# Moving chunk 3's first layer norm behind the first half's scaled queries in a convolution and attention kernel

## The chip, the cores and the metric

The kernel runs on one core of a Trainium2 chip. The metric is device time in microseconds of one execution. A core has TensorE (matrix multiply, with a queue of its own for weight loads), VectorE, ScalarE and GpSimd, and the sync engine, which here only starts transfers. Each engine works through its own list of instructions in the order in which they are written and waits for the others on semaphores.

## The reference

Two blocks in a row on x of shape (32, 32, 16, 16): 32 images of 32 channels and 16 x 16 pixels. The first block, cut to what matters here:

```python
def _biasfree_ln(x, w):
    mu = jnp.mean(x, axis=1, keepdims=True)
    var = jnp.mean((x - mu) ** 2, axis=1, keepdims=True)
    return x / jnp.sqrt(var + EPS) * w[None, :, None, None]

def _elgca_attn(x, dw_w, dw_b, qkvl_w, qkvl_b):
...
    x1, x2 = (x[:, :C2], x[:, C2:])
    x1 = _gelu(_conv(x1, dw_w, dw_b, groups=C2, pad=1))
    x2 = _gelu(_conv(x2, qkvl_w, qkvl_b))
    x2 = x2.reshape(B, HEADS, C4, H, W)
    q = jnp.sum(x2[:, :HEADS - 3], axis=1)
    k = x2[:, HEADS - 3]
    v = x2[:, HEADS - 2].reshape(B, C4, H * W)
    lfeat = x2[:, HEADS - 1]
    qf = _avg_pool_3s2p1(q).reshape(B, C4, -1)
    kf = _max_pool_2s2(k).reshape(B, C4, -1)
    qk = jnp.einsum('bcn,bdn->bcd', qf, kf)
    attn = jnp.swapaxes(jax.nn.softmax(qk, axis=1), 1, 2)
    out = jnp.einsum('bcd,bdn->bcn', attn, v).reshape(B, C4, H, W)
    return jnp.concatenate([x1, lfeat, out], axis=1)
...
h = _biasfree_ln(x, ln1_w)
h = _elgca_attn(h, dw_w, dw_b, qkvl_w, qkvl_b)
out = h + x
m = _biasfree_ln(out, ln2_w)
m = _elgca_mlp(m, fc1_w, fc1_b, pos_w, pos_b, fc2_w, fc2_b)
return out + m
```

Here C2 is 16 and C4 is 8: a 3x3 depthwise convolution of one half of the channels beside a 1x1 projection of the other half into q, k, v and lfeat. The MLP is a 1x1 to 128 channels, a depthwise 3x3 added to it, and a 1x1 back. The second block is attention over the 256 pixels of each image (32 channels, softmax over the query axis) with a residual.

## The kernel before

The 32 images lie as four groups of eight: partition = group x 32 + channel, and eight **slots** of 256 pixels along the free axis. Two slots are a **chunk** (0 to 3; 512 columns, one PSUM bank wide), and two chunks are a **half** H (0: slots 0 to 3, 1: slots 4 to 7). All is in 32-bit floats. PSUM is used as eight banks: LOW is banks 0 to 3, HIGH is 4 to 7.

Nothing schedules the work: each engine's list is written out by hand, and the semaphores carry the order between engines. The stages around the change are these.

- `centre(0, k, banks)` and `variance(0, k, banks)` (L286, L297) are 32x32 matmuls with a constant matrix. Each serves one chunk: four groups times two slots, 8 matmuls. TensorE then uses 8 of its 16 tiles of 32 x 32, since group g and slot s go to row tile g and column tile (g + s) mod 4 (for the variance the other way round).
- ScalarE squares the centred values (`square`, L707), and in `inverse_root` (L713, L716) takes a logarithm and then an exponential with scale -0.5, which gives 1/sqrt(var + eps). Both need the table set `exp_tables`; GELU needs `gelu_tables`, and each change of set is an ACT_TABLE_LOAD.
- VectorE multiplies (`normalise_input`, L879) into the padded buffer `npad`, raising the semaphore `normed[0]` by one for each slot, and splits the result by pixel parity (`split_parities`, L887).
- `qk(k, bank)` (L306) projects a chunk's queries and keys with full 128x128 matmuls, and `qk_act` (L720) applies GELU for one half at a time. `pool_queries` (L343) is the average pool as a matmul, `scale_queries` (L724) divides by 9, and `pool_keys` (L896) is the max pool on VectorE.
- `channel_scores` (L356) gives the channel attention's scores. `softmax_in` (L906, L907), `channel_exp` on ScalarE (L729) and `softmax_out` (L914 to L919) give the mixing weights `mix_w`.
- The depthwise convolution with the v and lfeat projections runs as taps: `attn_singles` (L317) for taps 4, 3 and 5, straight from `npad`, and `attn_pairs` (L331) for the six others in pairs, from a copy `npairs` that the sync engine's queue makes (`place_pairs`, which waits for `normed[0]` of the whole half). `attn_act` (L733) is their GELU, and `mix(H, banks)` (L369) combines all. `residual` (L926) adds x, and the second layer norm begins with `centre(1, ...)` (L286 again).

Every matmul of 32-bit floats stands in the trace as two records; so one tap for four slots (16 matmuls) is 32 records, on all 16 tiles.

ScalarE's order in this stretch is

```python
            inverse_root(0, 2, HIGH)
            inverse_root(0, 3, HIGH)
            act.preload_act_table_set(gelu_tables)
            qk_act(0, 4)
            act.preload_act_table_set(exp_tables)
            scale_queries(0, 5)
            channel_exp(0)
            act.preload_act_table_set(gelu_tables)
```

The channel scores of half 0 lie in banks 5 and 6. Bank 6 also holds chunk 3's variance, so that TensorE waits for chunk 3's logarithm (`log_ready[0]`, 4) ahead of them.

## Time and profile before

| | |
|---|---|
| median of 3 runs | 112.94 us (112.91 to 114.23) |
| profiled execution, its own time | 113.05 us |
| its span, first to last instruction | 111.3 us |
| TensorE matmul busy | 95.7 us, 86% |
| TensorE weight loads busy | 53.9 us, 48% |
| ScalarE busy | 86.2 us, 77% |
| VectorE busy | 76.3 us, 69% |
| GpSimd busy | 11.7 us, 11% |
| mean granted TensorE clock | 0.995 |

The span leaves 1.75 us of the execution's own time outside it. Busy shares are means over the whole span; the change lies in a stretch of some 15 us near its start, and what bounds that stretch is read from the timelines and the chain of waits. Overlapping matmuls make TensorE look busier than it is: in the timeline a group's time runs to the end of its last matmul, and the next group may start some hundredths earlier.

### The profile page before, as it was taken

The numbers are of one execution on the slowest core, as the hardware profiler recorded it, in microseconds if no ns is written. First come the engines' busy times: TensorE is split into PE (matmuls) and PEld (weight loads), VectorE is DVE, ScalarE is ACT, GpSimd is POOL, SyncE is SP. The second block draws the span as 40 slices with busy tenths as digits, with TensorE's granted clock in tenths as the row PEclk, the third lists the DMA queues.
The fourth block names the chain that finished last, engine by engine and source line by source line (L and its number), as shares of the span: only waits on it lengthen the run. The fifth ranks groups of instructions, "written<-read, shape, count | busy, mean of one in ns | idle before, by whom it ended". The sixth has DMA issues, their size and how long they took to land.

```text
span 111.3 us, 5328 instructions
## 1 busy us (share of the span) xinstructions
PE 95.7 (86%) x2424; PEld 53.9 (48%) x2424; DVE 76.3 (69%) x155; ACT 86.2 (77%) x203; POOL 11.7 (11%) x25
## 2 busy tenths in 40 slices
PE   0097699999969999989987999999999999997660
PEld 0023286865425567324443653576624665585320
DVE  0002997554749897999879889567471789889751
ACT  4048897797989639896569899869999868979950
POOL 7010000000000000000000003692000030004200
PEclk9999999999999999999999999999999999999998
DMA  2991053200000000000000000000000200020022
GB/s 53 229 377 52 0 219 112 119 0 6 6 0 9 0 9 6 0 6 6 0 6 0 6 6 0 0 6 6 6 0 6 94 0 6 0 93 4 0 95 99
DMA packets 2070, 4.56 MB, mean 41 GB/s; under 512 B 384, under 2 KB 640, under 8 KB 2048
## 3 DMA queue, kind: packets, MB, share of 16 engines
q1 hardware_dynamic: 1904, 4.20, 10.6%
q8 instruction: 19, 0.31, 1.2%
q10 hardware_dynamic: 144, 0.03, 0.2%
q14 instruction: 3, 0.02, 0.1%
HBM read 1.96 MB, written 1.05 MB: 27 GB/s over the span
## 4 chain that ended last, share of the span: by engine, by line
PE 62%; ACT 22%; DVE 6%; DMA 4%; issue 3%; ACTq 0%; DVEq 0%
PE ps L398 19%; ACT prob L787 5%; PE ps L488 5%; ACT hpad L738 5%; PE ps L446 4%; DMA first<-first_in 4%; PE ps L498 4%; PE ps L518 4%; PE ps L481 3%; ACT prob L774 3%; PE ps L415 3%; PE ps L286 3%; PE ps L382 3%; PE ps L423 2%; ACT swapped L733 2%
## 5 line engine op out<-in xcount | busy, mean ns | idle before, releaser
L398 PE MATMUL ps<-hpad,third 32*32 32x450 f32 (+2 forms) x864 | 38.9, 563 | 0.1
L787 ACT ACTIVATE prob<-ps,smax 128x256 f32<-128x256 f32 x56 | 25.7, 477 | 3.8 <-DVE smax L999 3.7
L952 DVE SCALAR_TENSOR_TENSOR unit<-hpad,third,unit 128x544 f32<-128x544 f32 x32 | 23.5, 789 | 0.0
L999 DVE TENSOR_REDUCE smax<-ps 128x2 f32<-128x512 f32 x26 | 16.6, 685 | 4.7 <-PE ps L498 2.9
L398 PEld LDWEIGHTS ps<-hpad,third 32*32 32x32 f32 x864 | 15.1, 103 | 8.7 <-issue 4.5
L263 POOL TENSOR_TENSOR v_tok<-v_tok,row_inv 128x256 f32<-128x256 f32 x7 | 4.7, 677 | 87.8 <-DVE row_inv L1009 87.8
L787 ACT ACTIVATION_READ_ACCUMULATOR prob<-ps,smax 128x1 f32 x56 | 11.7, 209 | 0.0
L738 ACT ACTIVATE hpad<-ps,third 128x1024 f32<-128x1024 f32 x8 | 8.7, 1116 | 2.9 <-PE ps L382 2.4
L879 DVE SCALAR_TENSOR_TENSOR npad<-x,first,rstd 128x256 f32<-128x256 f32 x8 | 3.5, 480 | 10.3 <-ACT rstd L716 10.3
L518 PE MATMUL ps<-prob,v_tok 128*32 128x256 f32 x128 | 8.2, 383 | 2.3 <-ACT prob L774 1.1
L707 ACT ACTIVATE swapped<-ps 128x512 f32<-128x512 f32 x8 | 4.5, 593 | 7.2 <-PE ps L286 7.2
L498 PE MATMUL ps<-rstd,swapped 32*32 32x256 f32 x192 | 8.9, 383 | 0.6 <-ACT prob L787 0.6
L286 PE MATMUL ps<-x,first 32*32 32x256 f32 x64 | 3.8, 628 | 5.7 <-DMA first<-first_in 5.7
L488 PE MATMUL ps<-rstd,swapped 32*128 32x256 f32 x80 | 7.3, 397 | 0.3 <-DVE rstd L969 0.3
L747 ACT ACTIVATE acc<-ps,third 128x512 f32<-128x512 f32 x12 | 7.3, 688 | 0.2 <-PE ps L398 0.2
L498 PEld LDWEIGHTS ps<-rstd,swapped 32*32 32x32 f32 x192 | 4.9, 103 | 4.2 <-ACT prob L787 2.9
L518 PEld LDWEIGHTS ps<-prob,v_tok 128*32 128x32 f32 x128 | 3.9, 109 | 6.4 <-issue 2.8
L446 PE MATMUL ps<-X,third 32*32 32x256 f32 x128 | 6.9, 381 | 0.0
L297 PE MATMUL ps<-swapped,first 32*32 32x256 f32 x128 | 5.2, 446 | 1.6 <-ACT swapped L707 1.5
L713 ACT ACTIVATE rstd<-ps,eps_col 128x512 f32<-128x512 f32 x8 | 5.4, 676 | 1.5 <-PE ps L297 1.5
L488 PEld LDWEIGHTS ps<-rstd,swapped 32*128 32x128 f32 x80 | 5.1, 184 | 2.7 <-issue 1.2
L382 PE MATMUL ps<-m,third 32*32 32x512 f32 x64 | 4.4, 598 | 1.1 <-ACT hpad L738 0.9
(87 smaller groups left out, 145.1 us busy)
## 6 DMA issues: line engine op xcount, KB each, us to landing
prob<-npad SPq DMA_DIRECT2D x4, 297.5 KB, 2.5
x<-x_in SPq DMA_DIRECT2D x4, 256.0 KB, 5.6
y<-m SPq DMA_DIRECT2D x3, 256.0 KB, 2.5
third<-third_in SPq DMA_DIRECT2D x1, 456.5 KB, 6.8
second<-second_in SPq DMA_DIRECT2D x1, 401.5 KB, 5.8
y<-m SPq DMA_DIRECT2D x2, 128.0 KB, 2.0
first<-first_in ACTq DMA_DIRECT2D x1, 33.0 KB, 4.9
```

What stands on the lines that cost most here:

```text
L286: last = pe.matmul(ps[quadrant(rotated(g, s)), banks[s % 4], 0:NPIX], c1("centre")[quadrant(g), :], slot((x, res1)[ln], s)[quadrant(g), :] ...
L382: last = pe.matmul(ps[quadrant(c), bank, :], c3("fc1_w")[quadrant(g), c * C:(c + 1) * C], m[quadrant(g), k, :], start=True, stop=True)
L398: last = pe.matmul(inside(pixels(ps[quadrant(rotated(r, g)), banks[g], :]), tap), c3("taps")[quadrant(r), tap * C:(tap + 1) * C], inside(p ...
L446: last = pe.matmul(ps[quadrant(rotated(g, s)), bank, half * NPIX:(half + 1) * NPIX], c3(w)[quadrant(g), :], slot(X, s)[quadrant(g), :], st ...
L488: last = pe.matmul(ps[:, banks[q], jt * NPIX:(jt + 1) * NPIX], slot(swapped, s)[quadrant(q), jt * P:(jt + 1) * P], slot(rstd, s)[quadrant( ...
L498: last = pe.matmul(ps[quadrant(c), banks[q], jt * NPIX:(jt + 1) * NPIX], slot(swapped, s)[quadrant(q), at:at + C], slot(rstd, s)[quadrant( ...
L518: last = pe.matmul(ps[quadrant(g), bank, 0:NPIX], v_tok[:, s, at:at + C], prob[:, G * (slot_turn(s) % PROBS) + g, jt * NPIX:(jt + 1) * NPI ...
L738: act.activation(padded(hpad, h_first(k, g), 4, CENTRE), two(banks).rearrange("p g (t y s) -> p (g t) y s", t=2, s=SIDE), ACT.Gelu, bias=c ...
L747: act.activation(acc_buf(k, g), ps[:, banks[g], :], ACT.Gelu, bias=c3("pos_b")[:, g:g + 1]).then_inc(conv_gelu, 1)
L787: last = act.activation(prob[:, G * (slot_turn(s) % PROBS) + g, jt * NPIX:(jt + 1) * NPIX], ps[:, banks[q], jt * NPIX:(jt + 1) * NPIX], AC ...
L952: dve.scalar_tensor_tensor(out=sums, in0=source, scalar=weight, in1=sums, op0=ALU.mult, op1=ALU.add).then_inc(unit_step, 1)
L999: dve.tensor_reduce(smax[:, s, 2 * q:2 * q + 2], ps[:, banks[q], :].rearrange("p (j i) -> p j i", j=2), AX_X, ALU.max, negate=True).then_i ...
```

## The change

Chunk 3's `inverse_root` moves on ScalarE from ahead of the first GELU table load to behind `scale_queries(0, 5)`. VectorE takes chunk 3's `normalise_input` and `split_parities` behind `softmax_in(0)`. TensorE's list changes in four ways: the single taps of half 0 are split in two by slots (0 and 1, then 2 and 3, by the new argument `slots`); those of slots 0 and 1 for taps 4 and 3 come ahead of the variances of chunks 2 and 3; the pairs of half 0 all come behind the channel scores; and the wait for chunk 3's logarithm stands ahead of `qk(2, 7)`. The channel scores of half 0 use banks 4 and 5. No instruction is added or dropped, and there are as many table loads as before.

```diff
--- before.py
+++ after.py
@@ -307,11 +307,11 @@
                                      c2("qk_w"), start=True, stop=True)
                 last.then_inc(qk_proj, 1)
 
-            def attn_singles(H, lo, hi, banks):
+            def attn_singles(H, lo, hi, banks, slots=range(G)):
 
                 for i in range(lo, hi):
                     tap = ATTN_SINGLES[i]
-                    for t in range(G):
+                    for t in slots:
                         s = G * H + t
                         for g in range(G):
                             pe.matmul(inside(pixels(ps[quadrant(rotated(g, s)), banks[t], 0:NPIX]), tap),
@@ -531,21 +531,23 @@
             centre(0, 2, HIGH)
             pe.wait_ge(x_loaded[3], 16)
             centre(0, 3, HIGH)
+            pe.wait_ge(second_loaded, 16)
+            pe.wait_ge(normed[0], 2)
+            attn_singles(0, 0, 2, LOW, (0, 1))
             variance(0, 2, HIGH)
             variance(0, 3, HIGH)
-            pe.wait_ge(second_loaded, 16)
-            pe.wait_ge(normed[0], 4)
-            attn_singles(0, 0, 1, LOW)
+            attn_singles(0, 2, 3, LOW, (0, 1))
             pe.wait_ge(log_ready[0], 3)
             qk(0, 4)
             qk(1, 4)
-            attn_singles(0, 1, 3, LOW)
+            pe.wait_ge(normed[0], 4)
+            attn_singles(0, 0, 2, LOW, (2, 3))
             pool_queries(0, 5)
-            attn_pairs(0, 0, 1, LOW)
+            attn_singles(0, 2, 3, LOW, (2, 3))
+            pe.wait_ge(kf_zeroed, 1)
+            channel_scores(0, (4, 5))
+            attn_pairs(0, 0, 3, LOW)
             pe.wait_ge(log_ready[0], 4)
-            pe.wait_ge(kf_zeroed, 1)
-            channel_scores(0, (5, 6))
-            attn_pairs(0, 1, 3, LOW)
             qk(2, 7)
             qk(3, 7)
             mix(0, LOW)
@@ -801,11 +803,11 @@
             square(0, 2, HIGH)
             square(0, 3, HIGH)
             inverse_root(0, 2, HIGH)
-            inverse_root(0, 3, HIGH)
             act.preload_act_table_set(gelu_tables)
             qk_act(0, 4)
             act.preload_act_table_set(exp_tables)
             scale_queries(0, 5)
+            inverse_root(0, 3, HIGH)
             channel_exp(0)
             act.preload_act_table_set(gelu_tables)
             act.wait_ge(second_loaded, 16)
@@ -1013,7 +1015,7 @@
                 dve.tensor_tensor(slot(m, s), ps[:, bank, 0:NPIX], slot(X, s), ALU.add).then_inc(y_ready, 1)
 
             dve.wait_ge(first_loaded, 16)
-            for k in range(CHUNKS):
+            for k in range(CHUNKS - 1):
                 dve.wait_ge(x_loaded[k], 16)
                 normalise_input(k)
                 if k == 0:
@@ -1021,7 +1023,10 @@
                 split_parities(k)
             dve.wait_ge(kf_zeroed, 1)
             pool_keys(0)
-            softmax_in(0, (5, 6))
+            softmax_in(0, (4, 5))
+            dve.wait_ge(x_loaded[3], 16)
+            normalise_input(3)
+            split_parities(3)
             dve.wait_ge(blocks_zeroed, 1)
             dve.wait_ge(mix_preset, 1)
             softmax_out(0)
```

How the lists look, first **TensorE** from the variances of chunks 2 and 3 (L297) on; L317 are single taps, L306 the projections, L343 the pooling of the queries, L331 the pairs. Before:

```order
15 L297 MATMUL ps<-swapped,first 32x256 [waits squared0]
16 L297 MATMUL ps<-swapped,first 32x256 x7
17 L317 MATMUL ps<-npad,second 32x256 [waits normed0,second_loaded]
18 L317 MATMUL ps<-npad,second 32x256 x15
19 L306 MATMUL ps<-second,parity 128x64 [waits parity_split,log_ready0]
20 L306 MATMUL ps<-second,parity 128x64 x3
21 L306 MATMUL ps<-second,parity 128x64 [waits parity_split]
22 L306 MATMUL ps<-second,parity 128x64 x3
23 L317 MATMUL ps<-npad,second 32x16x15 x32
24 L343 MATMUL ps<-qk_tok,second 128x64 [waits qk_gelu]
25 L343 MATMUL ps<-qk_tok,second 128x64 x3
26 L331 MATMUL ps<-prob,second 32x16x15 [waits pairs_placed0]
```

With the change:

```order
13 L317 MATMUL ps<-npad,second 32x256 [waits normed0,second_loaded]
14 L317 MATMUL ps<-npad,second 32x256 x7
15 L317 MATMUL ps<-npad,second 32x16x15 x8
16 L297 MATMUL ps<-swapped,first 32x256 [waits squared0]
17 L297 MATMUL ps<-swapped,first 32x256 x7
18 L297 MATMUL ps<-swapped,first 32x256 [waits squared0]
19 L297 MATMUL ps<-swapped,first 32x256 x7
20 L317 MATMUL ps<-npad,second 32x16x15 x8
21 L306 MATMUL ps<-second,parity 128x64 [waits parity_split,log_ready0]
22 L306 MATMUL ps<-second,parity 128x64 x3
23 L306 MATMUL ps<-second,parity 128x64 [waits parity_split]
24 L306 MATMUL ps<-second,parity 128x64 x3
```

Sixteen single-tap matmuls (two taps of two slots) now stand ahead of the variances, and eight more (the third tap) behind them, ahead of the projections L306; the wait for `normed0` that opens them is now for two slots and not for four. The list goes on:

```order
25 L317 MATMUL ps<-npad,second 32x256 [waits normed0]
26 L317 MATMUL ps<-npad,second 32x256 x7
27 L317 MATMUL ps<-npad,second 32x16x15 x8
28 L343 MATMUL ps<-qk_tok,second 128x64 [waits qk_gelu]
29 L343 MATMUL ps<-qk_tok,second 128x64 x3
30 L317 MATMUL ps<-npad,second 32x16x15 x8
31 L356 MATMUL ps<-qf,kf 32x8 [waits q_scaled,k_pooled,kf_zeroed]
32 L356 MATMUL ps<-qf,kf 32x8 x15
33 L331 MATMUL ps<-prob,second 32x16x15 [waits pairs_placed0]
34 L331 MATMUL ps<-prob,second 32x16x15 x15
```

The other two slots' singles stand around the pooling L343, and all 48 pair matmuls follow the channel scores L356; before, 16 of them stood ahead of the scores.

**ScalarE** from chunk 2's logarithm on (L713 and L716 before are L715 and L718 with the change, and L720, L724, L729, L733 become L722, L726, L731, L735). Before:

```order
10 L713 ACTIVATE rstd<-ps,eps_col 128x512 [waits var_ready0]
11 L716 ACTIVATE rstd<-rstd 128x512 [waits log_ready0]
12 L713 ACTIVATE rstd<-ps,eps_col 128x512 [waits var_ready0]
13 L716 ACTIVATE rstd<-rstd 128x512 [waits log_ready0]
14 L805 ACT_TABLE_LOAD
15 L720 ACTIVATE qk_tok<-ps 128x512 [waits qk_proj]
16 L807 ACT_TABLE_LOAD
17 L724 ACTIVATE qf<-ps 128x64 [waits q_pooled]
18 L729 ACTIVATE att<-att 128x32 [waits att_shifted]
```

With the change:

```order
10 L715 ACTIVATE rstd<-ps,eps_col 128x512 [waits var_ready0]
11 L718 ACTIVATE rstd<-rstd 128x512 [waits log_ready0]
12 L806 ACT_TABLE_LOAD
13 L722 ACTIVATE qk_tok<-ps 128x512 [waits qk_proj]
14 L808 ACT_TABLE_LOAD
15 L726 ACTIVATE qf<-ps 128x64 [waits q_pooled]
16 L715 ACTIVATE rstd<-ps,eps_col 128x512 [waits var_ready0]
17 L718 ACTIVATE rstd<-rstd 128x512 [waits log_ready0]
18 L731 ACTIVATE att<-att 128x32 [waits att_shifted]
```

One logarithm and one exponential have moved from ahead of the first table load to behind the scaled queries.

**VectorE** from chunk 3's normalisation (L879 before, L881 with the change) on. Before:

```order
13 L879 SCALAR_TENSOR_TENSOR npad<-x,first,rstd 128x16x16 [waits rstd_ready0,x_loaded3]
14 L879 SCALAR_TENSOR_TENSOR npad<-x,first,rstd 128x16x16
15 L887 TENSOR_SCALAR parity<-npad,second 128x128 [waits normed0]
16 L887 TENSOR_SCALAR parity<-npad,second 128x128 x3
17 L896 TENSOR_REDUCE kf<-qk_tok 128x4x8 [waits qk_gelu,kf_zeroed]
18 L896 TENSOR_REDUCE kf<-qk_tok 128x4x8
19 L906 TENSOR_REDUCE att_max<-ps 128x4 [waits att_scores]
20 L907 TENSOR_TENSOR att<-ps,att_max 128x32 [waits dve_chain]
21 L914 TENSOR_REDUCE att_sum<-att 128x4 [waits att_exp,mix_preset,blocks_zeroed]
```

With the change:

```order
13 L898 TENSOR_REDUCE kf<-qk_tok 128x4x8 [waits qk_gelu,kf_zeroed]
14 L898 TENSOR_REDUCE kf<-qk_tok 128x4x8
15 L908 TENSOR_REDUCE att_max<-ps 128x4 [waits att_scores]
16 L909 TENSOR_TENSOR att<-ps,att_max 128x32 [waits dve_chain]
17 L881 SCALAR_TENSOR_TENSOR npad<-x,first,rstd 128x16x16 [waits rstd_ready0,x_loaded3]
18 L881 SCALAR_TENSOR_TENSOR npad<-x,first,rstd 128x16x16
19 L889 TENSOR_SCALAR parity<-npad,second 128x128 [waits normed0]
20 L889 TENSOR_SCALAR parity<-npad,second 128x128 x3
21 L916 TENSOR_REDUCE att_sum<-att 128x4 [waits att_exp,mix_preset,blocks_zeroed]
```

Chunk 3's two multiplications and four splits now stand between the softmax's subtraction and its sum (L914 before, L916 with the change), so `mix_w` waits for them.

## Rows read from the trace of the kernel before

**Rows 1.** The chain of work that ended last, in order of time, 10 to 32 us (start us, us, what)

```profile
17.39 1.03 PE ps L343 x8
...
23.06 0.73 PE ps L369 x32
```

**Rows 2.** ScalarE's timeline, 10 to 31 us (start us, us, engine line op out<-in xcount)

```profile
12.72 0.69 ACT L713 ACTIVATE rstd<-ps,eps_col 128x512 f32<-128x512 f32 x1 [0.34 <-PE ps L297]
...
13.97 0.67 ACT L713 ACTIVATE rstd<-ps,eps_col 128x512 f32<-128x512 f32 x1
...
15.32 1.28 ACT L805 ACT_TABLE_LOAD   x1
16.62 0.60 ACT L720 ACTIVATE qk_tok<-ps 128x512 f32<-128x512 f32 x1
...
18.53 0.22 ACT L724 ACTIVATE qf<-ps 128x64 f32<-128x64 f32 x1
20.11 0.23 ACT L729 ACTIVATE att<-att 128x32 f32<-128x32 f32 x1 [1.36 <-DVE att L907]
...
21.65 1.26 ACT L733 ACTIVATE swapped<-ps,second 128x512 f32<-128x512 f32 x2
22.84 0.60 ACT L720 ACTIVATE qk_tok<-ps 128x512 f32<-128x512 f32 x1
```

**Rows 3.** TensorE's timeline, 11 to 24 us (same columns)

```profile
11.95 1.15 PE L297 MATMUL ps<-swapped,first 32*32 32x256 f32 x32 [1.45 <-ACT swapped L707]
13.37 0.73 PE L317 MATMUL ps<-npad,second 32*32 32x256 f32 x32 [0.26 <-DVE npad L879]
14.02 2.00 PE L306 MATMUL ps<-second,parity 128*128 128x64 f32 x16
15.95 1.44 PE L317 MATMUL ps<-npad,second 32*32 32x240 f32 x64
...
18.36 0.69 PE L331 MATMUL ps<-prob,second 32*32 32x240 f32 x32
19.11 0.37 PE L356 MATMUL ps<-qf,kf 64*32 64x8 f32 x32
19.41 1.47 PE L331 MATMUL ps<-prob,second 32*32 32x256 f32 x64
20.80 2.00 PE L306 MATMUL ps<-second,parity 128*128 128x64 f32 x16
```

**Rows 4.** VectorE's timeline, 10 to 31 us

```profile
10.32 0.88 DVE L879 SCALAR_TENSOR_TENSOR npad<-x,first,rstd 128x256 f32<-128x256 f32 x2 [10.32 <-ACT rstd L716]
...
16.24 0.87 DVE L879 SCALAR_TENSOR_TENSOR npad<-x,first,rstd 128x256 f32<-128x256 f32 x2
17.15 1.12 DVE L887 TENSOR_SCALAR parity<-npad,second 128x128 f32<-128x128 f32 x4
...
20.47 0.18 DVE L914 TENSOR_REDUCE att_sum<-att 128x4 f32<-128x32 f32 x1 [0.39 <-ACT att L729]
...
21.47 0.18 DVE L919 COPY mix_w<-att_turned 128x32 f32<-128x32 f32 x1
23.47 0.65 DVE L896 TENSOR_REDUCE kf<-qk_tok 128x32 f32<-128x128 f32 x2 [1.81 <-ACT qk_tok L720]
```

**Rows 5.** TensorE's timeline around two groups of L446, 88.8 to 90 and 93.89 to 95 us

```profile
88.88 1.07 PE L446 MATMUL ps<-X,third 32*32 32x256 f32 x16
...
93.90 1.12 PE L446 MATMUL ps<-X,third 32*32 32x256 f32 x32
```

**Rows 6.** DMA issues by line (KB each, median us to landing), and the second half's first pairs on TensorE

```profile
prob<-npad SPq DMA_DIRECT2D x4, 297.5 KB, 2.5
...
30.50 0.78 PE L331 MATMUL ps<-prob,second 32*32 32x240 f32 x32
```

**Rows 7.** TensorE's timeline, 24 to 29.5 us

```profile
26.96 0.42 PE L317 MATMUL ps<-npad,second 32*32 32x256 f32 x4
27.03 0.42 PE L297 MATMUL ps<-swapped,first 32*32 32x256 f32 x8
```

## The prediction

> **What bounds the kernel now.** I read the chain of waits first. From 10 to 25 us it runs along TensorE's list, and the two rows in [rows 1] are what a reader should see of it: the query pooling and the mixing matmuls each start when TensorE comes to them or when ScalarE releases them, with no slack to speak of. Then the timelines. ScalarE's shows that the first GELU (16.62) waits for its table load (15.32 + 1.28), and that load stands behind chunk 3's logarithm and exponential, which take from 13.97 to 15.32, so 1.35 us [rows 2]. That is what the change takes out of the way. TensorE's shows groups almost end to end: from the first projection at 14.02 to the end of the second pair of projections, 20.80 + 2.00 = 22.80, there is no hole of even 0.1 us except around the channel scores [rows 3]. ScalarE's second GELU then starts at 22.84 [rows 2]. So two engines are nearly late together: whatever ScalarE gives, TensorE's list must be able to take.
>
> **Step 1, the early single taps.** They need only chunk 0's normalisation, which ends at 10.32 + 0.88 = 11.20 [rows 4]. With the 0.15 that the mixing matmuls took to follow ScalarE's end (21.65 + 1.26 = 22.91 to 23.06) [rows 1, 2] they start at 11.35, in a hole that lasts until the variances at 11.95 [rows 3]. The group is 32 records, but on two slots, so on 8 tiles. The nearest rows: 32 records on 8 tiles of the same width took 1.12, and 16 records on 4 tiles took 1.07 [rows 5]. The double work costs nothing more, so it is the four records in a row on each tile that set the time: 0.26 each (1.05 to the start of what follows; these groups overlap the next by some 0.07). On all 16 tiles 64 records, again four on a tile, took 1.44, or 1.38 to the next group's start (15.95 to 18.36 less the pooling's 1.03) [rows 1, 3]. So the early group holds its tiles until about 12.40, and 0.45 of that is behind the point where chunk 2's variance could start. It shares four tiles with it. Bounds: no delay of the variance (its other tiles are free), or 0.85 (it waits for the whole group, priced at 1.44). I take 0.3: four records and then two of the variance on a tile are 6 x 0.26 = 1.56 from 11.35, 12.91 and a tail of 0.1, against the variance's end just ahead of the logarithm at 12.72 [rows 2]. Chunk 2's logarithm then starts at 13.03.
>
> A page bears on this. The Trainium skill, "TensorEngine Tiling (Array Packing)", Theoretical Speedup, has 32 x 32 tiles bring up to 16 times, so half the tiles in use is half the speed. That speaks against splitting the taps by slots. Taken literally from the 16-tile rows (0.34 a round and not 0.26) it would add 8 x 0.08 = 0.6 to the groups below; the trace shows a half-used array at 0.26 a round, so it agrees in direction and not in full size.
>
> **Step 2, the projections.** They wait for chunk 2's logarithm, 13.03 + 0.69 = 13.72, so start at 13.85, not 14.02; the third tap of slots 0 and 1 (16 records, two rounds) fits ahead, since the busiest tile has 8 rounds from 11.35, to 13.45. They take 15.95 - 14.02 = 1.93 [rows 3] and TensorE is free at 15.78. ScalarE: exponential to 14.38, table load to 15.68, GELU at 15.88 when the projections' last has ended, not 16.62 [rows 2]. So of 1.35 taken off ScalarE 0.74 arrives; TensorE keeps the rest.
>
> **Step 3, the pooling and the scores.** Ahead of the pooling stand the singles of slots 2 and 3, 32 records on 8 tiles, 1.05: to 16.83. GELU is done at 16.48, so the pooling is bound by TensorE: 16.83 and not 17.33 (0.50 of gain left). It ends at 17.87 after 1.03 [rows 1]. The third tap of these slots takes 0.55 (two rounds and a small gap), where 0.75 stood (18.36 to 19.11) [rows 3]; the scaled queries are ready at 17.97 + 0.22 = 18.19 [rows 2] and hide behind it. Scores at 18.42, not 19.11: gain 0.69. Their move to banks 4 and 5 costs nothing: both banks' readers, GELU and the scaling, are done before; if they kept banks 5 and 6, they would wait for the moved logarithm.
>
> **Step 4, where TensorE gives it back.** All pairs now follow the scores: 96 records where 64 took 20.80 - 19.41 = 1.39 and 32 took 0.65 to 0.75 [rows 3], so 2.05. Scores' 0.30, then 18.75 + 2.05 = 20.80. The second half's projections start at the same 20.80 as before. The whole gain on TensorE has gone into taps that now run on half the tiles.
>
> **Step 5, the new wait.** Chunk 3's layer norm: ScalarE takes it at 18.21 (its set of tables is the one loaded there, so no load is added) and ends 1.35 later, 19.56. `channel_exp`, queued behind it, is ready at 19.42 (before, it started at 20.11, which is 1.00 behind the scores' start) [rows 2, 3], so it is held by 0.14 and still far ahead of 20.11. VectorE starts chunk 3's normalisation at 19.70. From there to the end of the splits is 17.15 + 1.12 - 16.24 = 2.03 [rows 4]: 21.73. Two things wait for that. First `qk(3, 7)`: with the handover and a weight load it starts at 21.9, where TensorE would be ready at 21.77, and ends at 22.95, not 22.80. Second `softmax_out(0)`, now behind the splits on VectorE: 20.47 to 21.65 is 1.18 [rows 4], so `mix_w` is ready at 22.83, not 21.65; the mixing matmuls are behind the projections anyway, 22.95, so it hides by 0.1. If that cover goes it costs one for one. `attn_act` runs from 21.13 to 22.39 and is not late. The second GELU starts at 22.98, not 22.84: a loss of 0.14. VectorE's key pooling (23.47) [rows 4] follows it, then the residual and the second layer norm's centring, so all move by that 0.14.
>
> **Step 6, the rest.** The sync queue's copy for the second half's pairs waits for chunk 3, from 20.6 and not 17.1. With 2.5 to land and two issues it is there by about 25; its reader comes at 30.50 [rows 6], so it costs nothing. From 25 us on the lists are the same, and the shift goes through. Sum: +0.15 on an execution of 113.05, so 113.2; that execution lay 0.1 over the median of 112.94. **Forecast: 113.1.**
>
> **The rivals.** All of them lie inside 2%, which is about what a measurement of this kernel can tell from no change.
>
> *Faster: half-used tiles cost by the record.* If small groups keep the 16-tile price of 0.02 a record (0.65 for 32) [rows 3] and the variance is not held, the logarithm stays at 12.72, the third tap is done at 13.4, the projections end at 15.5 (VectorE's splits of chunk 1 bound them) and the pooling starts right behind GELU at 16.3. Chunk 3's norm then starts at 17.73, its splits end at 21.25, and the second GELU starts at 22.53: -0.3, so 112.6. For it: the change does take 1.35 us from the binding table load. Against it: 16 records on 4 tiles cost as much as 32 on 8 [rows 5].
>
> *Slower: the early taps hold up the variance.* If chunk 2's variance starts only when the 32 early records are through, and these cost 16-tile rounds, it starts at 11.35 + 1.44 = 12.79, and the logarithm at 13.55. From a logarithm at 13.2 on each hundredth moves the projections and all that follows, in the end chunk 3's splits: +0.5 on the forecast, so 113.6. Against it: in a like place matmuls of two lines are in the array together, L317 at 26.96 ahead of L297's last at 27.03, though L297 stands first in the list [rows 7]. The Trainium skill, "TensorE: Matmul & The Clock Gate", Part 3, has matmuls start and end strictly in order, and this rival is what such a queue would do here; the rows just named speak against it.
>
> *No effect of its own.* The order of instructions shows that the logarithm has left the place ahead of the table load, so that the change does nothing is not left open; what could change by another amount is the second half of the kernel, where I assume a plain shift.
>
> **How the numbers follow.** Forecast 0.50, with its own range 112.9 to 113.4; faster rival 0.23; slower rival 0.23; something else, beyond either, 0.04. The range runs from the one rival to the other with 0.15 to 0.2 on each side for the scatter between runs (112.91, 112.94, and 113.05 in the profile): 112.4 to 113.8. Over 2% faster would be under 110.7, over 2% slower over 115.2; no case reaches them, and the 0.04 is split: 0.01, 0.97, 0.02.
>
> **What would show it.** Right, if the profile of the changed kernel has the early singles at 11.3 to 11.4, chunk 2's logarithm near 13.0, the first GELU near 15.9 right behind the projections and no longer behind its table load, the pooling near 16.8 with no wait for GELU, the second half's projections near 20.8, a VectorE that sums the softmax only at 21.6, and the second GELU near 23.0. The rivals part at two rows: the logarithm (12.7 or 13.5) and the time of 32 singles on two slots (0.7 or 1.4 for my 1.1). I would be wrong if the pairs behind the scores took clearly less than 2.05, if `mix_w` and not the projections released the mixing, or if the shift at 25 us were not the shift at the end.

## The result, and the profile after

The changed kernel took 112.53 us (median of 20 executions, 112.06 to 113.87) against 113.56 for the kernel before (median of 20, 112.50 to 122.22). The ratio is 0.9948, with a 95% interval of 0.9925 to 0.9971: 0.6 us faster, between 0.3 and 0.9. That ratio leaves out executions that lie far over the fastest of their kernel; the medians keep them, and what is known of them is told with the experiments. By the bound of 2% this is no change. The profiled execution took 112.90 us with a span of 111.1.

The two spans can't be set against each other directly. The first loads land when they land: the first normalisation on VectorE starts at 10.32 in the trace before [rows 4] and at 9.54 in the one after. So times below are also given as **offsets** from that start, and the **stretch** is the time from it to the first fc1 GELU on ScalarE (L738 before, L740 after), 10.32 to 30.96 before, so 20.64.

ScalarE's timeline after the change, which answers to [rows 2]:

```profile
12.16 0.69 ACT L715 ACTIVATE rstd<-ps,eps_col 128x512 f32<-128x512 f32 x1 [0.56 <-PE ps L297]
...
13.53 1.28 ACT L806 ACT_TABLE_LOAD   x1
14.93 0.60 ACT L722 ACTIVATE qk_tok<-ps 128x512 f32<-128x512 f32 x1
...
16.96 0.22 ACT L726 ACTIVATE qf<-ps 128x64 f32<-128x64 f32 x1
17.08 0.68 ACT L715 ACTIVATE rstd<-ps,eps_col 128x512 f32<-128x512 f32 x1
...
21.77 0.60 ACT L722 ACTIVATE qk_tok<-ps 128x512 f32<-128x512 f32 x1 [0.57 <-PE ps L306]
...
29.89 2.12 ACT L740 ACTIVATE hpad<-ps,third 128x1024 f32<-128x1024 f32 x2
```

The table load now starts at 13.53, right behind chunk 2's exponential, and ends at 14.81; GELU at 14.93 waits for the projections and no longer for the load. Chunk 3's logarithm comes at 17.08, behind the scaled queries. The stretch is 29.89 - 9.54 = 20.35, so 0.29 shorter.

TensorE's timeline, which answers to [rows 3]:

```profile
10.56 1.05 PE L317 MATMUL ps<-npad,second 32*32 32x256 f32 x29 [0.90 <-DVE npad L881]
11.25 0.40 PE L297 MATMUL ps<-swapped,first 32*32 32x256 f32 x1
...
11.29 0.82 PE L297 MATMUL ps<-swapped,first 32*32 32x256 f32 x22
11.83 0.36 PE L317 MATMUL ps<-npad,second 32*32 32x240 f32 x1
...
12.90 2.00 PE L306 MATMUL ps<-second,parity 128*128 128x64 f32 x16 [0.17 <-ACT rstd L715]
14.82 1.07 PE L317 MATMUL ps<-npad,second 32*32 32x256 f32 x32
15.82 1.11 PE L343 MATMUL ps<-qk_tok,second 128*128 128x64 f32 x8
...
17.73 2.07 PE L331 MATMUL ps<-prob,second 32*32 32x240 f32 x96
19.74 2.00 PE L306 MATMUL ps<-second,parity 128*128 128x64 f32 x16
21.71 0.73 PE L369 MATMUL ps<-swapped,mix_w 32*32 32x256 f32 x32
```

A reader should see the early taps (L317 at 10.56) with the variances (L297, from 11.25 on) pushed in among their last (L317 at 11.83, which stands ahead of them in the list), and then groups end to end from 12.90 to 21.71. The 32 records on two slots take 1.00 to the next group's start (14.82 to 15.82), the 96 pairs 2.01 (17.73 to 19.74), and the mixing matmuls start when the second pair of projections is through.

VectorE's timeline, which answers to [rows 4]:

```profile
9.54 0.88 DVE L881 SCALAR_TENSOR_TENSOR npad<-x,first,rstd 128x256 f32<-128x256 f32 x2 [9.54 <-ACT rstd L718]
...
18.53 0.88 DVE L881 SCALAR_TENSOR_TENSOR npad<-x,first,rstd 128x256 f32<-128x256 f32 x2 [0.17 <-ACT rstd L718]
19.44 1.12 DVE L889 TENSOR_SCALAR parity<-npad,second 128x128 f32<-128x128 f32 x4
...
21.47 0.18 DVE L921 COPY mix_w<-att_turned 128x32 f32<-128x32 f32 x1
```

Chunk 3 is normalised at 18.53, its splits end at 19.44 + 1.12 = 20.56, and `mix_w` is ready at 21.65, 0.06 before the mixing matmuls at 21.71: it hides, barely.

One more row matters. At 75 us the changed kernel's lead over the trace before was 1.07 (0.78 of it from the earlier loads), and ten us later it was 0.15. In between stands this row of TensorE's:

```profile
75.82 0.37 PE L498 MATMUL ps<-rstd,swapped 32*32 32x256 f32 x1 [0.47 <-issue]
```

The hole of 0.47 before this row is put down to nothing that the profile shows ("issue"). Whether it belongs to the change is what the second experiment asks.

### The profile page after: what moved, and what is told of

Read it like the earlier page. It is cut to its first block, busy times and chain, and to the rows that moved or that the text cites. A ratio compares the mean times of both kernels' runs of the same rounds, so it can differ in the third digit from the quotient of the medians.

```text
span 111.1 us, 5328 instructions
## 1 busy us (share of the span) xinstructions
PE 96.8 (87%) x2424; PEld 54.4 (49%) x2424; DVE 76.4 (69%) x155; ACT 86.2 (78%) x203; POOL 11.7 (11%) x25
## 3 DMA queue, kind: packets, MB, share of 16 engines
HBM read 1.96 MB, written 1.05 MB: 27 GB/s over the span
## 4 chain that ended last, share of the span: by engine, by line
PE 64%; ACT 21%; DVE 5%; DMA 4%; issue 2%; SPq 0%; ACTq 0%; DVEq 0%
PE ps L398 18%; PE ps L498 5%; ACT prob L789 5%; PE ps L488 5%; ACT hpad L740 5%; PE ps L446 4%; DMA x<-x_in 4%; PE ps L518 4%; PE ps L306 4%; PE ps L481 3%; ACT prob L776 3%; PE ps L415 3%; PE ps L286 3%; PE ps L382 3%; PE ps L317 2%
## 5 line engine op out<-in xcount | busy, mean ns | idle before, releaser
L398 PEld LDWEIGHTS ps<-hpad,third 32*32 32x32 f32 x864 | 14.6, 103 | 9.9 <-issue 5.8
L740 ACT ACTIVATE hpad<-ps,third 128x1024 f32<-128x1024 f32 x8 | 8.7, 1115 | 2.9 <-PE ps L382 2.4
L881 DVE SCALAR_TENSOR_TENSOR npad<-x,first,rstd 128x256 f32<-128x256 f32 x8 | 3.5, 482 | 9.7 <-ACT rstd L718 9.7
L317 PE MATMUL ps<-npad,second 32*32 32x240 f32 (+1 forms) x192 | 6.3, 373 | 0.9 <-DVE npad L881 0.9
L446 PE MATMUL ps<-X,third 32*32 32x256 f32 x128 | 6.9, 381 | 0.0
L715 ACT ACTIVATE rstd<-ps,eps_col 128x512 f32<-128x512 f32 x8 | 5.4, 677 | 1.3 <-PE ps L297 1.3
L297 PE MATMUL ps<-swapped,first 32*32 32x256 f32 x128 | 5.7, 446 | 0.0
```

Source lines behind the costliest of these rows:

```text
L317: pe.matmul(inside(pixels(ps[quadrant(rotated(g, s)), banks[t], 0:NPIX]), tap), c2("attn_taps")[quadrant(g), i * C:(i + 1) * C], inside(pa ...
L398: last = pe.matmul(inside(pixels(ps[quadrant(rotated(r, g)), banks[g], :]), tap), c3("taps")[quadrant(r), tap * C:(tap + 1) * C], inside(p ...
L446: last = pe.matmul(ps[quadrant(rotated(g, s)), bank, half * NPIX:(half + 1) * NPIX], c3(w)[quadrant(g), :], slot(X, s)[quadrant(g), :], st ...
L740: act.activation(padded(hpad, h_first(k, g), 4, CENTRE), two(banks).rearrange("p g (t y s) -> p (g t) y s", t=2, s=SIDE), ACT.Gelu, bias=c ...
```

## The experiments

All ratios are to runs of the kernel before that were taken beside each kernel on the same chip; that chip was not the same for all of them. Of the edits the lines that matter are shown, and "..." marks what is left out.

**The two kernels again.** No edit.

> The kernel before, unchanged, to see how far one profile of it lies from the next. I measure a stretch inside the profile, from the start of chunk 0's normalisation on VectorE to the start of the first fc1 GELU on ScalarE: 10.32 to 30.96, so 20.64 us in the trace of before, and 9.54 to 29.89, so 20.35, with the change. If that stretch is what the change acts on, it repeats here at 20.6 within 0.05, the ratio is 1.00, and the first normalisation may start anywhere from 9.5 to 10.4, as the first loads land. The rival, that the stretch itself scatters by some tenths, would show another length here.

Ratio 1.0011 (0.9962 to 1.0059). The stretch was 21.32, not 20.64, so the rival has a point; two rows of TensorE's timeline show where:

```profile
18.86 1.72 PE L331 MATMUL ps<-prob,second 32*32 32x256 f32 x64
...
29.24 0.66 PE L317 MATMUL ps<-npad,second 32*32 32x240 f32 x20 [0.64 <-issue]
```

The second group of pairs took 1.72 where [rows 3] has 1.47, and the second half's single taps waited 0.64 for nothing visible. Offsets up to the channel scores are those of before within 0.01. The traces of the later experiments settle the rest. Four with the old order have a stretch of 20.63 to 20.65 (`before`, `before_late_copy`, `before_filled`, `before_filled2`), and four with the new order have 20.34 to 20.36 (`after`, `ctl_after2`, `after_warm`, `after_filled_warm`). So the stretch repeats to 0.02, but for stops of TensorE that come in some executions, and the new order is worth 0.29 in it.

> The changed kernel, unchanged. Stretch 20.35 again within 0.05; time 0.3 to 0.6 us under before. The profile of the change had a hole of 0.47 us on TensorE near 75.4 us that nothing explains, and the lead over before shrank there from 1.07 to 0.15. If that belongs to the new order of instructions it comes back here in the same place; if it is an accident of one execution it is gone, and this profile's span is about 0.8 us shorter from the first fc1 GELU to the end (81.2 in that profile, 80.3 in before's).

Ratio 0.9954 (0.9919 to 0.9988). Every offset up to the residual is that of the first trace after within 0.02. The hole at 75 us is gone: from the first fc1 GELU to the end 80.3, as before. So it does not come in every execution of the changed kernel, but it was no accident of one either: the trace of `after_late_copy`, told below, waits 0.44 for nothing visible ahead of the same instruction, 45.90 behind its first fc1 GELU (45.93 in the first trace after), and has 81.2 from there to the end, as that one had. The hole stands in 2 of 12 traces of kernels with any part of the change and in none of 6 without; that doesn't tell whether the change has a part in it. A smaller stop (0.41, in the second half's singles) made this stretch 20.56.

**One part of the change alone.** In the first kernel TensorE keeps the old order of taps and pairs, and ScalarE's and VectorE's lists are the new ones (the edit is to the changed kernel):

```diff
             centre(0, 3, HIGH)
-            pe.wait_ge(second_loaded, 16)
-            pe.wait_ge(normed[0], 2)
-            attn_singles(0, 0, 2, LOW, (0, 1))
             variance(0, 2, HIGH)
             variance(0, 3, HIGH)
...
+            attn_pairs(0, 0, 1, LOW)
             pe.wait_ge(kf_zeroed, 1)
             channel_scores(0, (4, 5))
-            attn_pairs(0, 0, 3, LOW)
+            attn_pairs(0, 1, 3, LOW)
```

> ScalarE's and VectorE's part of the change alone (and the banks and the later wait for the logarithm), with TensorE's taps in the old order. My theory: TensorE was nearly as late as ScalarE, so the GELU starts 0.5 earlier but the pooling does not, while chunk 3's norm now ends behind the scaled queries: splits end near 22.3 on the clock of the trace of before, second GELU near 23.4. The stretch is 0.5 to 0.7 longer than before's 20.64, time +0.5 to +0.7 us. Rival (ScalarE alone bounded the stage, the new tap order is of no use): the stretch is as short as with the whole change, 20.35, time -0.3 or better.

Ratio 1.003 (0.9992 to 1.0069): the gain is gone, as my theory has it, and the rival's 0.997 is excluded. The loss, 0.3 us, is under the 0.5 to 0.7 that I gave, and the interval includes 1.000. Its one profiled execution took 121.31 us, so that the forecast stretch was never seen undisturbed, and its granted clock says why (us, PE, PEld, DVE, ACT, POOL busy, PEclk, DMA share, GB/s):

```profile
10.00:12.00 2.00, 0.44 (x16) 0.18 (x16) 1.89 (x7) 1.96 (x4) 0.00 (x0) 1.00 0.04 8
12.00:14.00 2.00, 1.96 (x57) 0.50 (x48) 1.96 (x8) 1.62 (x3) 0.00 (x0) 0.59 0.00 0
14.00:24.00 10.00, 10.00 (x200) 7.50 (x185) 3.08 (x11) 4.41 (x7) 0.00 (x0) 0.50 0.16 63
...
38.00:40.00 2.00, 1.59 (x40) 0.37 (x36) 0.58 (x1) 1.99 (x2) 0.00 (x0) 1.00 0.00 0
```

The clock fell from 1.00 to 0.50, from 2.4 to 1.2 GHz, soon after 12 us and was not back until 36. Its matmuls show it, 1.17 and 3.67 where [rows 3] has 0.73 and 2.00:

```profile
12.98 1.17 PE L317 MATMUL ps<-npad,second 32*32 32x256 f32 x32
14.08 3.67 PE L306 MATMUL ps<-second,parity 128*128 128x64 f32 x16
```

In the second kernel ScalarE's and VectorE's lists are the old ones and TensorE's is the new one (again an edit to the changed kernel; VectorE's part is not shown):

```diff
             inverse_root(0, 2, HIGH)
+            inverse_root(0, 3, HIGH)
             act.preload_act_table_set(gelu_tables)
...
             scale_queries(0, 5)
-            inverse_root(0, 3, HIGH)
```

> TensorE's new order and banks 4 and 5 alone, with chunk 3's norm at its old place on ScalarE and VectorE. My theory: the early taps delay chunk 2's logarithm by 0.22 and with it the table load, and the pairs behind the scores come late: second GELU 0.5 to 0.7 later than before, time +0.5 to +0.7 us, so each part alone loses and only the two together gain. Rival (the early use of the hole is where the gain is from): the stretch is shorter than 20.64, time -0.2 or better.

Its stretch is 21.25, 0.61 longer than before's, as forecast. ScalarE's timeline:

```profile
12.32 0.69 ACT L715 ACTIVATE rstd<-ps,eps_col 128x512 f32<-128x512 f32 x1 [0.56 <-PE ps L297]
...
14.93 1.28 ACT L807 ACT_TABLE_LOAD   x1
16.22 0.60 ACT L722 ACTIVATE qk_tok<-ps 128x512 f32<-128x512 f32 x1
...
22.84 0.60 ACT L722 ACTIVATE qk_tok<-ps 128x512 f32<-128x512 f32 x1 [0.56 <-PE ps L306]
```

GELU again sits behind its table load, now 0.22 later by offset (6.52 for 6.30), and the second GELU is 0.62 later (13.14 for 12.52). But the time was only 1.0014 (0.9985 to 1.0043), where I had said 0.5 to 0.7 us more: 0.16 more, 0.45 better than its own stretch would have it. Its 12 executions lay within 0.7 us, where before's spread over 10. Its lowest is 113.16, 0.9 over before's lowest, 112.26; it is the others of before that are slower than its rows would have them. Something else than the order of the work had got better. It has the early taps.

**When the sync queue's copy starts.** A wait ahead of the second half's copy, in either kernel:

```diff
             place_pairs(0)
+            sp.wait_ge(qk_gelu, 2)
             place_pairs(1)
```

> The kernel before with one edit: the sync queue starts the second half's copy for the pairs only behind the second GELU (a wait for the second half's GELU), so 6 us later; its readers come 4 us after it lands. In the second trace of before the half-0 pairs had a stop of 0.25 us (1.72 for 1.47) and TensorE a hole of 0.64 in the second half's singles, while those copies held the DMA engines at 260 to 440 GB/s; the two traces of the change had no such stop in the pairs. Theory: TensorE's instructions come by DMA, and in before these copies fall where TensorE uses up 64 short matmuls and waits for more; the change moves them 2.3 us back, beside the slow projections, and that is the part of its gain that a clean trace does not show. Then this kernel is 0.2 to 0.4 us faster than before (ratio 0.997), with no stop in the half-0 pairs (1.47). Rival (the stops are accidents that have nothing to do with the copies): ratio 1.000 and stops as often.

> The changed kernel with the same late copy. By the theory there is less to gain, since the change has already moved the copy off the half-0 pairs: -0.4 to -0.7 us against before, within 0.1 of the change itself (-0.55). Rival: the same number, for another reason; so this one tells only whether the copy in its new place still costs something (then it would be 0.2 or more faster than the change).

The ratios are 0.9978 (0.9948 to 1.0007) and 0.997 (0.9941 to 0.9998). In the first the pairs took their plain 1.47 and the stretch was 20.65, though TensorE still stopped for 0.23 in the second half's singles (at 28.16). Its ratio is where the theory put it, but the interval holds 1.000, and 3 of its 12 executions still took 118.34 to 122.71. The second is no better than the change was on another chip. The copies may have a part in TensorE's small stops; they don't explain the gain.

The trace of the second, of an execution of 114.72 us, shows something else. It has the early taps, and yet its stretch is 21.64, 1.29 longer than the clean 20.35. Its rows of TensorE, and the engines' busy times from 12 to 13 us with the granted clock (the third figure from the end, 1.00):

```profile
11.12 1.51 PE L318 MATMUL ps<-npad,second 32*32 32x256 f32 x24 [1.00 <-DVE npad L882]
...
12.58 1.59 PE L298 MATMUL ps<-swapped,first 32*32 32x256 f32 x28
```

```profile
12.00:13.00 1.00, 1.00 (x39) 0.89 (x27) 1.00 (x3) 0.17 (x1) 0.00 (x0) 1.00 0.06 16
```

The early taps take 1.51 for 24 records, where the first trace after has 1.05 for 29, and the 32 records of the variances go from 12.26 to 14.17, where it has 11.25 to 12.32; the projections from 14.72 on take the plain 2.00. Before the first normalisation, matmuls of that width are slow in every trace without idle work: single records take 0.63 at 8.47 in the trace before and 0.37 to 0.40 at 11.25 in the trace after, at a granted clock of 1.00 both times. So here TensorE came to its full pace only near 14 us, and the granted clock of the profile does not show it.

**How many taps ahead of the variances.** `attn_singles(0, 0, n, LOW, (0, 1))` ahead of them and the rest behind, with n = 0 and n = 3 for the change's 2 (both edits are to the changed kernel):

> The changed kernel without early taps: all three single taps of slots 0 and 1 behind both variances. By my price of 0.26 us a round on 8 tiles the logarithm of chunk 2 goes back to 2.40 behind the first normalisation (2.62 with the change) but the projections wait for six rounds of singles and start at 4.3 to 4.4, not 3.36, and all behind them moves by 0.9: pairs of projections at 11.1, stretch 21.2 to 21.3 for 20.35, time +0.3 to +0.4 us against before. Rival (half-used tiles cost by the record, 0.02 each): 48 records take 1.0, projections at 4.0, stretch 20.9, time about as before.

> The changed kernel with all three single taps of slots 0 and 1 ahead of the variances, 48 records. By my price of 0.26 a round the tiles shared with chunk 2's variance have 8 rounds, so its logarithm starts 0.4 to 0.5 later than with the change (3.05 for 2.62 behind the first normalisation), the projections at 3.8 for 3.36, second GELU 12.65 for 12.23, stretch 20.8; time about +0.1 to +0.2 against before. Rival (the variance's matmuls overtake the taps in the array): logarithm at 2.65 and stretch 20.35, as with the change.

With n = 0 the ratio was 1.0032 (0.9984 to 1.0079), near my forecast, but the interval holds 1.000, and the rows that I forecast were not seen: its profile has no clean stretch (22.56), because the clock fell here too, right behind a hole on TensorE that the early taps would have filled:

```profile
11.00:12.00 1.00, 0.26 (x12) 0.21 (x16) 1.00 (x4) 1.00 (x3) 0.00 (x0) 1.00 0.00 0
12.00:13.00 1.00, 1.00 (x39) 0.67 (x29) 0.96 (x4) 0.41 (x2) 0.00 (x0) 0.53 0.07 16
...
16.00:17.00 1.00, 1.00 (x12) 1.00 (x10) 0.16 (x1) 0.00 (x0) 0.00 (x0) 1.00 0.00 0
```

With n = 3 the ratio was 1.0051 (1.0014 to 1.0088), 0.5 to 0.6 us more than before where I had said 0.1 to 0.2. The offsets are as forecast, the logarithm at 3.09 and the projections at 3.83; the second GELU at 12.79 (12.65) and the stretch at 20.92 (20.8) are 0.1 over. ScalarE's rows, with the normalisation at 9.69:

```profile
12.78 0.69 ACT L714 ACTIVATE rstd<-ps,eps_col 128x512 f32<-128x512 f32 x1 [1.02 <-PE ps L297]
```

So the price of a round on half-used tiles held, 0.23 to 0.26, and the taps do hold up the variance that shares their tiles. The rival in which the variance overtakes them falls. The 0.1 over, and part of the time, may belong to that execution: it took 114.17, its granted clock was 0.95 from 9.5 us to the end, and from the first fc1 GELU to the end it needed 81.8 for 80.3. The clock went down ahead of the taps (10.72), and of the other 11 executions one, of 113.99, had it too.

**The first pair tap ahead of the scores again**, with the rest of the change kept (an edit to the changed kernel):

```diff
             attn_singles(0, 2, 3, LOW, (2, 3))
+            attn_pairs(0, 0, 1, LOW)
             pe.wait_ge(kf_zeroed, 1)
             channel_scores(0, (4, 5))
-            attn_pairs(0, 0, 3, LOW)
+            attn_pairs(0, 1, 3, LOW)
```

> The changed kernel with the first pair tap ahead of the channel scores again, as before the change. TensorE's sum stays the same, but the scores come 0.65 later (8.53 for 7.88 behind the first normalisation), VectorE must take the softmax's first steps before chunk 3's normalisation, so the splits end 0.6 later and the last projection waits for them: second GELU 0.45 to 0.6 later than with the change (12.23), stretch 20.8 to 20.95, time 0 to +0.1 against before. Rival (the order of pairs and scores is free because TensorE's sum decides): stretch 20.35 as with the change.

Stretch 20.89, of which a stop in the second half's singles (0.34) is a part; second GELU 12.64, at the lower edge of the forecast. The ratio is 1.0032 (1.0000 to 1.0064), 0.36 us where I had said 0 to 0.1. VectorE takes the softmax's steps 0.67 later by offset (9.08 for 8.41) and the splits after them:

```profile
18.86 0.19 DVE L909 TENSOR_REDUCE att_max<-ps 128x4 f32<-128x32 f32 x1 [2.33 <-PE ps L356]
...
20.11 1.12 DVE L890 TENSOR_SCALAR parity<-npad,second 128x128 f32<-128x128 f32 x4
```

TensorE's pair of projections takes 2.35 for 2.00, because its second waits for those splits:

```profile
20.03 2.35 PE L306 MATMUL ps<-second,parity 128*128 128x64 f32 x16
```

This is the new wait of my step 5, shown where it bites; the pairs behind the scores are what keeps it off in the change.

**Filling the hole, and nothing else.** In the kernel before, 16 centring matmuls whose result nothing reads:

```diff
             centre(0, 3, HIGH)
+            pe.wait_ge(log_ready[0], 1)
+            for _ in range(2):
+                for t in range(2):
+                    for g in range(G):
+                        pe.matmul(ps[quadrant(rotated(g, t)), t, 0:NPIX], c1("centre")[quadrant(g), :],
+                                  slot(x, t)[quadrant(g), :], start=True, stop=True)
             variance(0, 2, HIGH)
```

> The kernel before with 16 more matmuls (32 records, 1.05 us) of the centring kind, whose result nothing reads, into banks 0 and 1 in the hole of TensorE between chunk 3's centring and chunk 2's variance; nothing else is changed. Two traces of kernels without the early taps show TensorE's clock falling to half right behind that hole (at 12.05 for 3.4 us, and at 12.35 for 23.9 us, that execution took 121.3 us); no trace with the early taps does. Theory: part of what the change gains, beyond the 0.29 of a clean trace, is that its early taps fill the hole, so that the clock does not fall. Then this kernel, with no reordering at all, has the stretch of before in a clean trace (20.64), no execution near 121, and a ratio of 0.997 to 0.998. Rival (the gain is all from the order of the work): ratio 1.000, and executions near 121 as often as before.

All 12 executions lay between 112.40 and 112.78. Of the 37 of the unfilled kernel beside them, 9 were over 116 and 7 more over 114. Those 16 are not in the ratio, which was 0.9996 (0.9985 to 1.0007), so on this chip my 0.997 was wrong: only 2 of the 21 that are in it were over 113.2. The clean stretch is 20.63. A second time, on the chip of the changed kernel:

> The kernel before with the hole near 11 us filled, again, now on the same chip as the changed kernel. Scatter within 0.5 us again and none near 121. If the order of the work is worth what the clean traces say, this is 0.25 to 0.35 us slower than the changed kernel's fast runs without a late or fallen clock; if the change gains by its order all that was measured (0.55), it is that much slower.

> The changed kernel again: lowest executions 0.25 to 0.35 us under the lowest of before and of the filled before; ratio to before 0.994 to 0.998, depending on how often before's clock falls on this chip. Some executions 1 us above its lowest, since its clock can still rise late (one trace had it at 14.1), but none near 121.

Filled: 0.9977 (0.9950 to 1.0004), 112.34 to 112.80, median 112.67. Changed: 0.9964 (0.9935 to 0.9994), 112.18 to 113.29, median 112.47; their stretches are 20.64 and 20.36. TensorE's rows of the filled kernel (L538 is the filler), with no hole between it and the variances:

```profile
9.69 1.99 PE L538 MATMUL ps<-x,first 32*32 32x256 f32 x28
11.59 1.15 PE L297 MATMUL ps<-swapped,first 32*32 32x256 f32 x32
```

So on one chip the order of the work is worth 0.1 (means) to 0.2 us (medians), with about 0.2 of uncertainty, beside 0.28 in the traces; filling the hole alone gives 0.26 of the change's 0.41 by these ratios, though its interval holds 0. The lowest executions lie closer than the 0.25 to 0.35 that I had said: 112.18 changed, 112.34 filled, 112.27 before.

Over all runs the count is plain. Kernels that keep the hole (the kernel before on every chip, `ctl_before`, `act_part`, `before_late_copy`, `early_0` and, told next, `before_warm`) had 48 of 224 executions over 116 us. Kernels with early taps or the filler in it had 1 of 153, and that one (127.02, at a granted clock of 0.76) is of `after_warm`, told next.

What the long executions are is less plain. For 43 of the 48 the mean granted clock is on record. In 30 it was 0.72 to 0.97, most often 0.90, as in the trace of `act_part`. In 13, of 119.74 to 122.86 us, it was 0.993 to 1.000, so the profile shows no fall in them. A full pace that comes late, as in `after_late_copy`, would look like that; no trace of such a long execution was taken, so this stays open. The same holds for the shorter scatter. Of the 99 executions of the kernel before that are in the ratios of the experiments, 30 were over 113.2, and only 2 of these (113.35 and 113.66) had a granted clock under 0.99. The one execution of that kind that was profiled, `ctl_before` with 113.31 at 0.999, has two stops of TensorE and no fall. The filler ends all of it, 24 of 24 executions within 0.5 us; by what way it ends the stops isn't shown.

**Idle work during the loads.** Five 128x128x256 matmuls of ones into bank 7 ahead of the first wait (VectorE sets the ones first; that is not shown):

```diff
+            pe.wait_ge(idle_set, 1)
+            for _ in range(5):
+                pe.matmul(ps[:, 7, 0:NPIX], idle[:, 0:P], idle[:, :], start=True, stop=True)
             pe.wait_ge(first_loaded, 16)
```

> The changed kernel with five 128x128x256 matmuls of ones into bank 7, whose result nothing reads, while the first loads are on their way. In the traces the clock rises only 8.9 to 14.1 us after the start, and until then 32x256 matmuls take 0.63 us instead of 0.37. If work during the load raises the clock earlier, the first centrings and variances run at 0.37: the first normalisation comes 0.5 to 0.9 us sooner behind the first centring (4.6 to 4.8 in the traces so far), and the time is 1.0 to 1.4 us under before. Rival (the clock rises no sooner, or falls again while TensorE waits for the loads): -0.5 like the change.

> The kernel before with the same five matmuls during the load. If the clock rises earlier this gains 0.5 to 0.9 us as in the changed kernel, and the difference between the two is what the order of the work alone is worth, which by the clean traces is 0.29. The hole near 11 us is still there, so executions near 121 us may still come. Rival: what the change gains over before is not 0.3 but 0.5 also with an early clock.

The changed kernel with it: 0.9933 (0.9896 to 0.9970), 0.76 us under before where I had said 1.0 to 1.4, median 111.76, one of 12 at 127.02. The kernel before with it: 0.9969 (0.9920 to 1.0018), but 6 of 12 over 120, all at a granted clock of 0.90. Without it 9 of 37 were over 116. The hole at 11 us may do more harm when TensorE came to its full pace earlier; 6 of 12 is too few to show it. The difference between the two cannot be read as I had meant to.

> The changed kernel with 8 idle matmuls (16 records, 0.55 us) in what is left of the hole, between chunk 3's centring and the early taps. If its remaining scatter comes from the clock rising late or falling there, the scatter shrinks to 0.5 us and the mean is 0.1 to 0.3 better than the changed kernel's; the lowest execution stays where it is. Rival: the hole left (0.9 us) is too short to matter, same mean.

> Both idle fillers: five matmuls of ones during the loads, 8 in the hole. The early clock took the trace of after_warm to a first normalisation 0.1 to 0.9 sooner and that kernel to 0.9933; with the hole filled as well its one execution at 127 and the upper ones at 112.5 should go. Ratio to before 0.988 to 0.992, the fastest of all, scatter under 0.8 us. Rival (the loads, not the clock, set when the work begins): no better than after_filled.

With 8 idle matmuls in what is left of the hole (in its trace they end at 10.58, 0.14 ahead of the early taps, where the first trace after shows 0.90 idle) the changed kernel took 0.9977 (0.9947 to 1.0006), no better than without: the rival holds, and the rest of the hole is too short to matter. With both it took 0.9940 (0.9904 to 0.9976), 111.19 to 112.80, the fastest on that chip, though its interval overlaps the changed kernel's. I had said 0.988 to 0.992 with a scatter under 0.8; it is slower than that and scatters over 1.6. There the 8 ran ahead of the hole, done at 9.25 with 1.04 idle behind them, so this kernel is in effect `after_warm` again. TensorE's first rows, L288 being the first centrings:

```profile
1.18 4.15 PE L527 MATMUL ps<-idle 128*128 128x256 f32 x10 [1.18 <-DVE idle L1028]
5.52 1.20 PE L288 MATMUL ps<-x,first 32*32 32x256 f32 x32 [0.19 <-DMA first<-first_in]
```

The idle work takes 4.15 while the loads are under way, and the 32 records of centring behind it 1.20 from 5.52; TensorE's timeline before has the same 32 at 1.80 from 5.69. So idle work during the loads brings TensorE to its full pace earlier.

## Why the prediction was wrong

The range (112.4 to 113.8) holds the time, 112.53, but I forecast 0.15 more than before and the kernel is 0.3 to 0.9 faster. Two steps failed. The sum of steps 1 to 5 was 0.43 too dear, the largest part of it (0.15) in step 5's new wait, which did not come: the second GELU came 0.29 earlier and not 0.14 later. And TensorE's scatter around the hole near 11 us, which the early taps mostly end, stood in no step at all.

The path was right, and a trace can be laid beside it. As offsets from the first normalisation, forecast (the prediction's times less 10.32), measured after, and before:

| | forecast | after | before |
|---|---|---|---|
| chunk 2's logarithm | 2.71 | 2.62 | 2.40 |
| projections | 3.53 | 3.36 | 3.70 |
| first GELU | 5.56 | 5.39 | 6.30 |
| pooling | 6.51 | 6.28 | 7.00 |
| channel scores | 8.10 | 7.88 | 8.79 |
| second half's projections | 10.48 | 10.20 | 10.48 |
| end of chunk 3's splits | 11.41 | 11.02 | 7.95 |
| second GELU | 12.66 | 12.23 | 12.52 |

**Step 1** was right in kind: the early taps delay the logarithm, by 0.22 and not 0.31. **Step 2** charged 0.13 for the handover from the logarithm to the projections, and it took 0.05 (12.16 + 0.69 to 12.90). **Steps 3 and 4** priced 32 records on 8 tiles at 1.05 and the pairs at 2.05, measured 1.00 and 2.01; the gain up to the second half's projections, which I let vanish to 0, is 0.28. **Step 5** failed as put: "with the handover and a weight load it starts at 21.9, where TensorE would be ready at 21.77". The splits end 0.39 earlier than I had them by offset, and the second projections take the plain 2.00 with no wait inside them. I had charged ScalarE 0.24 between the scaling and the logarithm, which overlap (0.12), on top of what came from ahead. `pair_ahead` shows that the wait is real, 0.35, once the scores come later. So the terms were too dear in a row: the logarithm by 0.09, the handover by 0.08, the pooling and its handovers by 0.06, the taps and pairs by 0.06, the wait of step 5 by 0.15, each put at its safe value. With roundings they make the 0.43 between 12.66 and 12.23, three times the 0.14 (12.66 less 12.52) on which the sign hung.

**Step 6**, a plain shift for the rest, holds: from the first fc1 GELU to the end it is 80.3 to 80.4 in 15 of the 18 traces. The others are the two with the hole near 75 us (81.2) and `early_3` (81.8).

What had no step at all is how steadily TensorE runs. I read its mean granted clock in the trace before, 0.995, and took it for given; the early taps were to me 0.45 us in the way of the variance. They also fill a hole after which some executions go slow. Two traces of kernels without them (`act_part`, `early_0`) show the clock fall to 0.50 right behind the hole, and none of those with them or a filler shows that, though `early_3` has 0.95 and `after_late_copy` a full pace that came late. The filler alone takes the kernel before to 0.9977 on the chip where the change has 0.9964, and to 0.9996 on another. So of the 0.4 to 0.6 us timed, 0.29 is what the traces show for the order, and I put the rest down to the end of the scatter, which the filler gives too. That falls of the clock are the cause of the rest is not shown, and the granted clocks on record speak against it for all but 2 of the 99 executions that count; the stops and the late pace are left, and they stay open.

**The faster rival** gave the right size, 112.6, by a wrong way: small groups do not cost by the record, and the logarithm did move. That my range held the time is luck of the same kind: this rival set its lower end. **The slower rival** is excluded by the logarithm, 2.62 behind the first normalisation where it had 3.23, and shown in part by n = 3. The variances start at 11.25, while taps that stand ahead of them in the list still start at 11.83. The Trainium skill, "TensorE: Matmul & The Clock Gate", Part 3, has TensorE start and end its matmuls in strict order; these starts don't agree with it, and the measurement decides. Open is the share of the order in the timed gain, 0.1 to 0.3 us.

## What to carry to other kernels

When two engines are nearly late together, moving work off one is worth nothing until the other's list is refitted too: neither half of this change gained by itself (1.003 and 1.0014, both intervals holding 1.000; the one clean trace of a half is 0.61 longer), and together they gain. When the forecast is a sum of many small terms whose sign hangs on a tenth or two, take each at its middle and not at its safe end, and say that the sign is open. And look at where TensorE stands idle early in a kernel before pricing what fills it: filling the hole may be worth as much as the work it brings forward.

## What the runs showed of the hardware

After holes of 1.9 and 2.1 us on TensorE near 11 us, its granted clock fell from 1.00 to 0.50: for 24 us in one trace (`act_part`), with 128x64 projections at 3.67 us for 2.00, and for 3 us in the other (`early_0`). After holes of 1.1, 1.5, 1.7 and 2.0 us in the same place four other traces show no fall. With 16 matmuls of no use in the hole, 24 of 24 executions lay within 0.5 us of each other, where the kernel without them spread over about 10.

The granted clock in the profile does not show all of TensorE's pace: 32x256 records took 0.63 at the start of a trace and 0.37 to 0.40 later, at 1.00 both times, and 13 executions of 119.74 to 122.86 us had a mean of 0.993 to 1.000.

A stream of small matmuls costs neither by the record nor by the tile: 32 records of single taps on 8 tiles took 1.00 to the next group's start, 64 on all 16 tiles 1.37, and 32 on 16 tiles 0.65 [rows 3]. Half the tiles cost 1.5 times as much for the same work, not twice and not the same.

TensorE also stops now and then for 0.2 to 0.6 us with nothing to wait for, most often inside the second half's single taps and in two traces at the same instruction near 75 us. That is as large as the effect studied here, so one trace each could not have settled it.
